# Attention stage of a convolution and attention kernel: sums of three slots at a time, a ring of four buffers for the exponentials, the last 64 keys stored inside the fourth block of keys, and the copy of the sums moved to ScalarE

## The reference, cut to what matters

```python
def _L1_attn_ref(x, att_w, ...):            # x: layer-normed tokens, (4, 3136, 64)
    wa, wb, wc = (att_w[:F], att_w[F:2 * F], att_w[2 * F:])
    a = einsum('bif,f->bi', x, wa)
    b = einsum('bjf,f->bj', x, wb)
    c = einsum('bif,bjf->bij', x * wc, x)
    scores = a[:, :, None] + b[:, None, :] + c
    attn_weight = softmax(scores, axis=2)
    attn = einsum('bij,bjf->bif', attn_weight, x)
    ...                                     # gates of x and attn
```

## Time and profile before

| | us |
|---|---|
| median of three runs | 1970.3 |
| the profiled execution | 1970.36 |
| its span | 1968.2 |
| PE busy | 1712.3 (87%) |
| DVE busy | 1227.8 (62%) |
| ACT busy | 1160.4 (59%) |
| POOL busy | 665.3 (34%) |

### The profile page before, as it was taken

How to read it: one execution, slowest core, us unless ns; L and a number is a source line. 1 busy time by engine, 2 the same in 40 slices (tenths; PEclk the granted TensorE clock), 3 DMA queues, 4 the chain that set the end, 5 groups by cost and what they waited for, 6 DMA issues and landing times. The chain is left out here.

```text
span 1968.2 us, 33809 instructions
## 1 busy us (share of the span) xinstructions
PE 1712.3 (87%) x13187; PEld 626.5 (32%) x13187; DVE 1227.8 (62%) x1835; ACT 1160.4 (59%) x1568; POOL 665.3 (34%) x392
## 2 busy tenths in 40 slices
PE   4468778778765789999999999999987999999998
PEld 1011111111111434433443343444344334433333
DVE  3249999999996566666666666666365345453433
ACT  2799989999922434444444444444454546566564
POOL 0798978988641310000000000000030113332222
PEclk9799999999987679999999999999986999999999
DMA  2121211211230210000000000100021000010000
GB/s 97 82 103 44 83 43 42 83 54 34 81 129 21 98 34 15 15 15 15 14 13 15 13 15 15 48 15 16 15 84 33 8 5 8 8 40 8 7 10 9
DMA packets 27711, 73.27 MB, mean 37 GB/s; under 512 B 6968, under 2 KB 16184, under 8 KB 26160
## 3 DMA queue, kind: packets, MB, share of 16 engines
q1 hardware_dynamic: 27424, 70.31, 11.2%
q10 hardware_dynamic: 144, 0.96, 0.1%
HBM read 47.84 MB, written 13.62 MB: 31 GB/s over the span
## 5 line engine op out<-in xcount | busy, mean ns | idle before, releaser
L1142 ACT ACTIVATE at_prob<-at_ps_s 128x896 f32<-128x896 f32 x336 | 304.8, 917 | 361.0 <-PE at_ps_s L1029 353.0
L1292 DVE TENSOR_REDUCE at_mpart<-at_ps_m 128x1 f32<-128x384 f32 (+3 forms) x800 | 396.4, 556 | 119.3 <-PE at_ps_m L1007 90.0
L424 DVE TENSOR_TENSOR cm_prod<-cm_ps_ev,win 128x1792 f32<-128x1792 f32 x196 | 388.3, 2018 | 13.4 <-ACT cm_ps_ev L475 9.5
L368 POOL TENSOR_TENSOR cm_diff<-front 128x1792 f32<-128x1792 f32 x98 | 320.6, 3275 | 69.1 <-POOLq L113 39.0
L1814 ACT ACTIVATE ge_hid<-ge_ps,ffn 128x448 f32<-128x448 f32 x448 | 249.3, 633 | 123.0 <-PE ge_ps L1681 123.0
L1045 PE MATMUL at_ps_a<-at_prob,win 128*64 128x448 f32 x1344 | 295.8, 554 | 0.0
L581 PE MATMUL cm_ps_acc<-cm_prod,cst 128*32 128x504 f32 x1568 | 218.9, 631 | 76.0 <-DVE cm_prod L424 45.8
L1029 PE MATMUL at_ps_s<-vh,front 64*128 64x448 f16 x1344 | 252.1, 352 | 2.9 <-DMA vl<-at_mrow 2.9
L1029 PE MATMUL at_ps_s<-vl,front 64*128 64x448 f16 x1344 | 251.2, 351 | 0.0
L946 POOL TENSOR_TENSOR attn<-attn 64x448 f32<-64x448 f32 x28 | 31.6, 1129 | 528.7 <-DMA attn<-attn 528.7
L1658 PE MATMUL ge_ps<-ge_hid,ffn 128*64 128x448 f32 x896 | 194.3, 555 | 0.5 <-DVE ge_part L1992 0.4
(11 more groups left out here) (221 smaller groups left out, 1871.4 us busy)
## 6 DMA issues: line engine op xcount, KB each, us to landing
win<-x_dram SPq DMA_DIRECT2D x28, 868.0 KB
at_rden<-rden_dram SPq DMA_DIRECT2D x28, 224.0 KB, 3.3
x_dram<-win SPq DMA_DIRECT2D x4, 962.0 KB
conv_out<-cm_cout SPq DMA_DIRECT2D x28, 112.0 KB, 4.0
win<-x SPq DMA_DIRECT2D x2, 1568.0 KB, 12.2
t_dram<-front SPq DMA_DIRECT2D x2, 1568.0 KB, 6.8
attn<-attn SPq DMA_DIRECT2D x28, 112.0 KB, 2.2
front<-t_dram SPq DMA_DIRECT2D x2, 1568.0 KB, 9.0
```

The lines of the kernel that those rows point to most:

```text
L368: pool.tensor_tensor(diff[:, s % ND, 0:n, :].rearrange("p n (r c) -> p n r c", c=W), a.rearrange("p n (r c) -> p n r c", c=W), b, ALU.subt ...
L424: v.tensor_tensor(prod[:, hs, :, 0:CH].rearrange("p s (r c) -> p s r c", c=W), ev.rearrange("p s (r c) -> p s r c", c=W), wv, ALU.mult).th ...
L1142: act.activation(prob_of(s)[0:w, 0:a, :], ps_s[0:w, (s + 1 - par) % 2, 0:a, 0:CH], ACT.Exp).then_inc(exp_done, 1)
L1292: v.tensor_reduce(mpart[0:w, a, part:part + 1], ps_m[0:w, j % RB, 0:rough_columns(e)], AX.X, ALU.max).then_inc(rough_max, 1)
```

## The change

Four things change, all in the attention stage.

The sums are done for three slots at a time: those of slots 0 to 2 before slot 4, 3 to 5 before slot 7, 6 to 8 before slot 10, and 9 to 12 in slot 1 of the next body. The ring of exponentials has four buffers in place of three, and slot 12's scores now also wait for the exponentials of slot 10.

Rough scores have their second place of a slot in every third slot (before the next group of sums) in place of every second.

The last 64 keys stand in the key buffer behind the fourth quarter of the first half of the keys, so a rough score over them is one matmul of 448 columns in place of two. The rows of ones of the key buffer are written from a short row of 96, read repeatedly.

The copy of a block's sums out of PSUM is done by ScalarE at the beginning of slot 1's exponential, in place of VectorE after its sixth maximum.

```diff
+        LOW = HALF_KEYS + LAST
+        END = slice(HALF_KEYS, LOW)
+        STRETCH = 96
...
-        BLOCK_AT, INVERT_AT = 5, 13
+        BLOCK_AT, INVERT_AT = 1, 13
...
-        NP = 3
+        TOGETHER = 3
+        NP = TOGETHER + 1
...
-        ones_row = sb("at_ones_row", [2, HALF_KEYS], F16)
+        ones_row = sb("at_ones_row", [2, STRETCH], F16)
...
-            at = [(s, p) for s in range(SL) for p in ((0, 2) if s % 2 == 0 else (0,))]
+            at = [(s, p) for s in range(SL) for p in ((0, 2) if s % TOGETHER == 0 else (0,))]
...
-                            sp.dma_start(xs[row:row + 1, 2 * t + i, 0:HALF_KEYS],
-                                         ones_row[0:1, :]).then_inc(spread[2 * t + i], 16)
+                            sp.dma_start(xs[row:row + 1, 2 * t + i, 0:HALF_KEYS].rearrange("p (a n) -> p a n", n=STRETCH),
+                                         ones_row[0:1, :].unsqueeze(1).broadcast_to([1, HALF_KEYS // STRETCH, STRETCH])) \
+                                .then_inc(spread[2 * t + i], 16)
...
-                    ins = pe.matmul(ps_m[0:w, j % RB, 0:KEYS], queries, xs[rows, b, kb * KEYS:(kb + 1) * KEYS],
-                                    start=True, stop=True, tile_position=(64 * half, 0))
-                    if part == PARTS - 2:
-                        ins = pe.matmul(ps_m[0:w, j % RB, KEYS:KEYS + LAST], queries, xs[rows, b, 2 * HALF_KEYS:PIX],
-                                        start=True, stop=True, tile_position=(64 * half, 0))
-                    ins.then_inc(rough_done, 1)
+                    n = rough_columns(e)
+                    pe.matmul(ps_m[0:w, j % RB, 0:n], queries, xs[rows, b, kb * KEYS:kb * KEYS + n], start=True, stop=True,
+                              tile_position=(64 * half, 0)).then_inc(rough_done, 1)
...
-                    if part == 0 and s < SL - 1 and not (n == 0 and s < 2):
+                    if part == 0 and not (n == 0 and s < 2):
                         pe.wait_ge(exp_done, n * SL + s - 1)
...
-                        if attend and s >= LAG + 1 and (s % 2 == 1 or s == SL - 1):
-                            for back in range(s - LAG - s % 2, s - LAG + 1):
+                        if attend and s > TOGETHER and s % TOGETHER == 1:
+                            for back in range(s - LAG - TOGETHER + 1, s - LAG + 1):
...
-                            for back in range(SL - LAG, SL):
+                            for back in range(SL - LAG - 2, SL):
...
+                def block_out(n, par):
+                    act.wait_ge(sum_done, n * SL + SL)
+                    act.wait_ge(divided, n + 1)
+                    act.copy(stage[:, par, :], ps_a[:, 0:CH]).then_inc(sums_out, 1)
...
+                        if s == BLOCK_AT and step not in ((0, 0), (0, 1)):
+                            block_out(i - 2, par)
...
-                        if j == BLOCK_AT and i > 1:
-                            block_out(i - 2, par)
```

More of the change, by code:

```diff
@@ L867, in stack @@
                         for row in (C - 1, 2 * C - 1):
-                            sp.dma_start(xs[row:row + 1, 2 * t + i, 0:HALF_KEYS],
-                                         ones_row[0:1, :]).then_inc(spread[2 * t + i], 16)
-                        sp.dma_start(xs[C - 1:C, 2 * t + i, 2 * HALF_KEYS:PIX],
-                                     ones_row[0:1, 0:LAST]).then_inc(spread[2 * t + i], 16)
+                            sp.dma_start(xs[row:row + 1, 2 * t + i, 0:HALF_KEYS].rearrange("p (a n) -> p a n", n=STRETCH),
+                                         ones_row[0:1, :].unsqueeze(1).broadcast_to([1, HALF_KEYS // STRETCH, STRETCH])) \
+                                .then_inc(spread[2 * t + i], 16)
+                        sp.dma_start(xs[C - 1:C, 2 * t + i, END], ones_row[0:1, 0:LAST]).then_inc(spread[2 * t + i], 16)
                     sp.wait_ge(split, NG + t)
@@ L879, in stack @@
                                          hi[t][64 * i:64 * i + C - 1, keys]).then_inc(spread[b], 16)
-                            sp.dma_start(xs[64 * half:64 * half + 64, b, HALF_KEYS:2 * HALF_KEYS],
+                            sp.dma_start(xs[64 * half:64 * half + 64, b, LOW:PIX],
                                          lo[t][64 * i:64 * i + 64, keys]).then_inc(spread[b], 16)
-                        sp.dma_start(xs[0:C - 1, b, tail], hi[t][64 * i:64 * i + C - 1, tail]).then_inc(spread[b], 16)
-                        sp.dma_start(xs[64:128, b, tail], lo[t][64 * i:64 * i + 64, tail]).then_inc(spread[b], 16)
+                        sp.dma_start(xs[0:C - 1, b, END], hi[t][64 * i:64 * i + C - 1, tail]).then_inc(spread[b], 16)
+                        sp.dma_start(xs[64:128, b, END], lo[t][64 * i:64 * i + 64, tail]).then_inc(spread[b], 16)
                 def maxima(b, q):
@@ L1021, in scores @@
                         half = vl if part else vh
-                        ins = pe.matmul(bank[0:LAST, 0, :], xs[:, m, 2 * HALF_KEYS:PIX], half[:, m, columns_of(k)],
+                        ins = pe.matmul(bank[0:LAST, 0, :], xs[:, m, END], half[:, m, columns_of(k)],
                                         start=(part == 0), stop=(part == 1))
@@ L1027, in scores @@
                                 rows = slice(64 * a, 64 * a + 64)
-                                at = part * HALF_KEYS + s * TT
+                                at = part * LOW + s * TT
                                 ins = pe.matmul(bank[:, a, :], xs[rows, m, at:at + TT], half[rows, m, columns_of(k)],
@@ L1112, in _ @@
                 plain_steps(body)
-                for s in range(SL - LAG, SL):
+                for s in range(SL - LAG - 2, SL):
                     for a in range(len(tiles(s))):
@@ L1187, in _ @@
                 steps(act, body)
+                last = B * NCH - 1
+                block_out(last, last % 2)
             @block.vector
@@ L1271, in _ @@
                 ones(0)
[L1273 to L1276, removed]
                 def invert(n):
@@ L1320, in _ @@
                 last = B * NCH - 1
-                block_out(last, last % 2)
                 invert(last)
```

## The result

The changed kernel takes 1979.89 us, the median of five runs (1979.39 to 1984.84), against 1971.12 us for the kernel before in five runs on the same chip (1969.34 to 1972.25). The ratio is 1.0049, 95% interval 1.0038 to 1.0061: 9 us slower, against 20 forecast.

The account below looks back on a forecast made before the run. PE's in-order program was taken to bound the attention stage. The terms -11 - 14 - 4 + 27.9 + 12 + 6.5 + 1.0 + 1.8 = +20 us, on a median of 1970.3, gave 1990 us; the eight-in-ten range was 1972 to 2003.

Parts of the forecast that it names:

- The end of a block: Transpose to the next body's scores: sums no longer cover the chain over VectorE and DMAs, so PE waits; +27.9 us.
- The second chain: Projection, ScalarE's rounding, VectorE's remainder, first maximum: holds the next body's fourth rough score, 0.43 us more in common blocks.
- The copy off VectorE: Slot 2: without the copy on VectorE, a pair's second rough score no longer waits; -0.53 us a block, -14 us.
- The inversion: Slot 6: VectorE's 0.45 us inversion now delays the bank that a rough score needs; 0.46 us a block, +12 us.
- Rough scores in one matmul: Rough scores over the last keys: 92 extra matmuls go; 0.15 us a block, -4 us.
- Sums in threes, the switching: Fewer groups of sums on PE, so less switching between kinds of matmul; 0.42 us a block saved, -11 us.
- Exponentials: Third slot of scores in a row waits for the first one's exponential; 0.24 us a block, +6.5 us.
- A common block: Time between transposes in a common block: from 25.5 to 25.9 us, +0.38.
- the two marks that the prediction set itself: Time between transposes of a common block: 25.9 us would show the forecast right, under 25.3 us wrong.
- The waits cancel half: Rival: groups save 0.7 and the inversion costs nothing, block ends as forecast; 1970 us, chance 0.06.
- VectorE and ScalarE keep up: Rival: in slots 3 to 6 and at the fourth rough score, banks are freed in time; 1964 us, chance 0.10.
- The clock falls: Rival: waits at the ends of twelve blocks drop PE to 1.2 GHz, 48 us on top; 2038 us, chance 0.04.

Follow-up runs that it names:

- experiment 6: Changed kernel with the sums of slots 9 and 10 put back between the transpose and the next body, before slot 12's scores: 1953.07 us, ratio 0.9914.
- experiment 9: Changed kernel with one row of maxima sent instead of two, so half the DMAs (second half of the keys' scores lack their maximum): 1966.27 us, ratio 0.9975.
- experiment 5: Changed kernel with the inversion of the denominators after the twentieth maximum instead of the fourteenth, which also moves the second body's token split: 1975.08 us, ratio 1.0023.
- experiment 8: Changed kernel with sums of slots 9 and 10 back before slot 12's scores and the inversion after the twentieth maximum: 1943.15 us, ratio 0.9860.
- experiment 10: Changed kernel with the rough scores' second places in every second slot again, in the very first body alone: 1988.76 us, ratio 1.0092.
- experiment 4: Kernel before with the copy on ScalarE and the last keys inside the fourth block, sums still in pairs of slots: 1957.30 us, ratio 0.9927.
- experiment 11: Changed kernel with the copy of the sums back on VectorE after the sixth maximum: 1999.74 us, ratio 1.0142.
- experiment 1: Kernel before with only the copy of a block's sums moved, to ScalarE in slot 1 from VectorE after its sixth maximum: 1956.85 us, ratio 0.9929.
- experiment 3: Kernel before with only the rough score over the last keys changed, to one matmul of 448 columns instead of two: 1971.33 us, ratio 1.0001.

## Why the prediction was right, and where it was off

The way and the mechanism were right: slower, because the sums no longer cover the chain from the transpose to the next body's scores. The size was forecast at 20 us and is 9. Step by step:

- *The end of a block*, +27.9 forecast. Undoing it gave 26.8 (experiment 6; 25.8 counted through the kernel before). The chain was 3.01 to 3.21 us in all bodies with two DMAs and 4.36 to 4.40 with four, as read from two places before. The second chain is real (experiment 9) but adds less: from transpose to sums 4.33 us, forecast 4.31 + 0.26 = 4.57. 0.10 of this is the transpose, which holds PE 0.20 and not 0.30, the rest the first maximum, which follows the start of VectorE's remainder closer than in the earlier trace rows (0.60 and 0.74).
- *The copy off VectorE*, -14: -14.3 alone, -19.9 in the new order. Right, and a little small.
- *The inversion*, +12 or 0.46 a block: 0.30 a common block in experiment 5, 0.34 in experiment 8, so 8 to 9 us. The medians of the two edits, 4.8 and 9.9, also hold the moved split and, in experiment 5, falls of the clock.
- *Rough scores in one matmul*, -4: nothing. The nearest row was a duration, and here a duration of 0.19 beside a running neighbour was no time of PE's.
- *Sums in threes, the switching*, -11: the transpose before scores takes 0.20, not 0.30, which is 0.1 x 27 = 3 us more gain. The price of a group held: three slots take 2.41 us (1133.44 to 1135.85), as 0.18 + 3 x 0.74 = 2.40 has it.
- *Exponentials*, +6.5: no experiment takes them alone, so this term stays open.
- *Not in the sum at all*: the very first body has no scores, only rough pairs between transposes of tokens, and the new places shorten it: 6.4 us between the two traces, 8.9 in the median of experiment 10. The prediction costed the places only in bodies with scores. This term put at nothing is the step that failed, and the largest part of the 11 us between forecast and result. The split in the second body is missing from the sum too, with the other sign: 3.2 us of wait where it was 2.1 at most.

The parts can also be added another way. Copy and last keys were forecast at -18 us and gave -13.9 (experiment 4); the rest of the change was forecast at +38.2 and, on top of those two, gave 8.8 + 13.9 = 22.7. Of the 15.5 us that this is short, the first body is 8.9 and the bodies with scores about 7; the missing gain of the keys hides 4 of them. That these errors partly cancel is luck.

A common block came out at 25.45 us, as before, where +0.38 was forecast; this lies between the two marks that the prediction set itself (25.9 for right, 25.3 for wrong). 0.24 of the 0.38 is the end of the block (4.33 for 4.57, transpose included) and 0.16 the inversion (0.30 for 0.46); the keys, which gave nothing, pull 0.15 the other way; the 0.13 left isn't placed.

The rival *The waits cancel half* (1970) came as near in time as the forecast, but not for its reason: the inversion does stall. *VectorE and ScalarE keep up* is refuted for VectorE by experiments 5, 8 and 11. *The clock falls*, which had 0.04, did happen in the trace, at a small price. One body of the last image, PE's timeline:

```profile
1256.53 0.36 PE L1030 MATMUL at_ps_s<-vh,front 64*128 64x448 f16 x2 [2.00 <-DMA vl<-at_mrow]
...
1257.56 4.17 PE L1046 MATMUL at_ps_a<-at_prob,win 128*64 128x448 f32 x12
1261.56 0.92 PE L1046 MATMUL at_ps_a<-at_prob_last,win 128*64 128x448 f32 x2
1262.40 0.34 PE L1012 MATMUL at_ps_m<-front,vh 64*128 64x384 f16 x2
```

and the window sums over it (busy of PE, PEld, DVE, ACT, POOL, then clock, DMA share, GB/s):

```profile
1256.40:1257.40 1.00, 0.87 (x10) 0.41 (x10) 0.00 (x0) 0.00 (x0) 0.00 (x0) 1.00 0.90 163
1257.40:1262.40 5.00, 5.00 (x18) 1.47 (x14) 1.02 (x2) 0.92 (x1) 0.00 (x0) 0.66 0.69 289
1262.40:1275.00 12.60, 12.44 (x101) 5.62 (x102) 8.78 (x20) 6.03 (x7) 1.67 (x2) 1.00 0.10 29
```

Behind 2.00 us of idle the first scores still run at full clock (1.00), then the sums run at 0.66 of it, partly at 1.2 GHz, and take 1262.40 - 1257.56 = 4.84 us instead of 3.15; then the clock is back. In the last body the scores behind the wait are slow already:

```profile
1411.71 0.55 PE L1030 MATMUL at_ps_s<-vh,front 64*128 64x448 f16 x2 [2.75 <-DMA vl<-at_mrow]
```

The changed kernel's profile has four such groups of sums, 5.0 us too long together, three behind waits on the DMA (1.59, 2.00 and 2.75 us) and one behind the 3.18 us wait on VectorE. That is about what its profiled execution has over the median (that these are the same microseconds is not shown). The traces of the kernel before and of experiments 1, 3, 4, 8 and 9 have none. The Trainium skill (TensorE: Matmul & The Clock Gate, section HAM oscillation) has the direction right; that every such wait would do it is not what the traces show: in the changed kernel waits of 1.57 and 1.56 us passed without a fall, in experiment 10 those of 2.00 and 2.75, in experiment 9 the one of 3.2 on VectorE.

## What to carry to other kernels

Work that stands between a request and the wait for its answer is cover: before moving it, measure the chain under it, and look for a place where it is already bare. An engine that is busy for six tenths can still hold the path at the one spot where its queue is dense; moving the copy to another engine was worth 14 us, moving the inversion to where something long follows 8 to 9. Grouping the matmuls by kind pays once both are done: a common block takes 24.93 us with the copy alone moved (experiment 1) and 24.52 to 24.56 in experiment 8. Go through the special first and last iterations of a changed schedule too, and look what else a constant places: here the first body gave the largest difference from the forecast, and one constant moved two jobs.

## What the runs showed of the hardware that was not expected

A matmul of 64 columns over one half of the array, recorded at 0.19 us and issued while the other half was at work, cost no more than the same 64 columns inside the matmul ahead of it (experiment 3). The granted clock can fall behind a wait whose first scores still ran at full clock (1256.4 to 1257.4 us: 1.00, 1257.4 to 1262.4: 0.66), and within one execution it fell behind one wait of 1.59 us and not behind those of 1.57 and 1.56.
